# Sampling offsets of a deformable convolution: grid added by a matmul, copies merged, products and batch norm operations reordered

## The reference

```
out = relu(group_norm(conv1x1(x, w1)))                 # 64 channels
om  = conv3x3(out, w_off, pad=1) + b_off               # 27 channels
off_x, off_y, mask = om[:, :9], om[:, 9:18], sigmoid(om[:, 18:])
py = grid_y + off_y ; px = grid_x + off_x              # grid: pixel + tap offset
sampled = bilinear_sample(out, py, px) * mask          # 9 taps per pixel
out = relu(group_norm(einsum(sampled, w2)))
x = relu(group_norm(conv1x1(out, w3)) + x)
...
_bn(x, g, b, m, v):  inv = g * rsqrt(v + eps);  x * inv + (b - m * inv)
```

## Time and profile before

| what | value |
|---|---|
| median of 3 runs | 91.75 us (91.61 to 92.53) |
| the profiled execution | 92.51 us |
| its span in the trace | 90.7 us |
| mean granted TensorE clock | 0.987 |
| busy: PE / DVE / ACT / POOL | 75.6 / 65.4 / 50.7 / 5.0 us |
| busy: PE's weight loads | 51.2 us |

### The profile page before, as it was taken

How to read it: one execution, slowest core, us unless ns; L and a number is a source line. 1 busy time by engine, 2 the same in 40 slices (tenths; PEclk the granted TensorE clock), 3 DMA queues, 4 the chain that set the end, 5 groups by cost and what they waited for, 6 DMA issues and landing times.

```text
span 90.7 us, 2168 instructions
## 1 busy us (share of the span) xinstructions
PE 75.6 (83%) x885; PEld 51.2 (56%) x885; DVE 65.4 (72%) x178; ACT 50.7 (56%) x91; POOL 5.0 (6%) x10
## 2 busy tenths in 40 slices
PE   4999999996899898999999998979579877776400
PEld 1325665565699797799896975443224474552100
DVE  1125449999999699996699617988884884848950
ACT  4101374779957999994874014509380254735760
POOL 7500110000000000000001300000000000000000
PEclk9999999999999999999999999999999999999995
DMA  2999800000000000000000000000000000000076
GB/s 27 311 322 316 335 3 0 0 7 0 0 7 0 0 7 0 4 11 0 0 7 0 0 0 7 0 0 0 0 0 0 0 0 0 0 11 0 0 248 215
DMA packets 3274, 4.17 MB, mean 46 GB/s; under 512 B 256, under 2 KB 2688, under 8 KB 3264
## 3 DMA queue, kind: packets, MB, share of 16 engines
q1 hardware_dynamic: 2992, 3.76, 12.8%
q10 hardware_dynamic: 272, 0.26, 0.8%
HBM read 2.98 MB, written 1.05 MB: 44 GB/s over the span
## 4 chain that ended last, share of the span: by engine, by line
PE 52%; DVE 29%; ACT 11%; issue 4%; DVEq 0%; ACTq 0%
PE acc L482 15%; PE slot L469 9%; DVE g_rows L893 8%; PE slot L361 6%; PE acc L609 5%; PE acc L372 3%; ACT g_cols L794 3%; PE slot L397 3%; PE acc L588 3%; ACT g_cols L707 2%; DVE g_cols L1039 2%; PE slot L546 2%; ACT pad L760 2%; DVE g_cols L992 2%; DVE stats L956 2%
## 5 line engine op out<-in xcount | busy, mean ns | idle before, releaser
L893 DVE TENSOR_TENSOR g_rows<-hats 128x2304 f32<-128x2304 f32 (+1 forms) x12 | 20.6, 1753 | 0.1
L707 ACT ACTIVATE g_cols<-slot 128x768 f32<-128x768 f32 x24 | 17.8, 830 | 3.7 <-PE slot L469 3.7
L482 PE MATMUL acc<-g_cols,v_sb 128*64 128x128 f32 x288 | 17.9, 276 | 0.0
L361 PE MATMUL slot<-zeros 128*128 128x512 bf16 x58 | 16.1, 412 | 1.2 <-DVE zeros L813 1.2
L482 PEld LDWEIGHTS acc<-g_cols,v_sb 128*64 128x64 f32 x288 | 15.5, 137 | 1.1 <-issue 0.3
L469 PE MATMUL slot<-consts_sb,g_rows 64*128 64x64 f32 x288 | 11.8, 226 | 2.1 <-DVE g_rows L893 1.7
L469 PEld LDWEIGHTS slot<-consts_sb,g_rows 64*128 64x128 f32 x288 | 10.3, 140 | 3.9 <-DVE g_rows L893 2.6
L361 PEld LDWEIGHTS slot<-zeros 128*128 128x128 bf16 x58 | 5.8, 108 | 8.0 <-issue 2.9
L760 ACT ACTIVATE pad<-g_cols 64x256 bf16<-64x256 int8 x8 | 3.3, 418 | 5.5 <-DVE g_cols L1039 5.4
L824 DVE BATCH_NORM_STATS2 stats<-acc 128x6 f32<-128x256 f32 x4 | 1.7, 430 | 5.1 <-PE acc L372 2.7
L397 PE MATMUL slot<-feat,woff_sb 128*64 128x256 f32 x36 | 4.7, 385 | 0.0
(11 more groups left out here) (140 smaller groups left out, 115.7 us busy)
## 6 DMA issues: line engine op xcount, KB each, us to landing
out<-g_cols SPq DMA_DIRECT2D x4, 256.0 KB, 2.3
x_sb<-x SPq DMA_DIRECT2D x3, 256.0 KB, 4.2
wq_sb<-wq SPq DMA_DIRECT2D x1, 484.5 KB, 5.9
woff_sb<-woff SPq DMA_DIRECT2D x1, 288.0 KB, 5.1
w_sb<-w SPq DMA_DIRECT2D x1, 288.0 KB, 5.2
x_sb<-x ACTq DMA_DIRECT2D x1, 256.0 KB, 3.3
w_sb<-w SPq DMA_DIRECT2D x1, 256.0 KB, 6.1
consts_sb<-consts SPq DMA_DIRECT2D x1, 232.0 KB, 5.1
```

What stands on the lines that cost most here:

```text
L361: nc.tensor.matmul(bank, zeros[:, 0:P], zeros[:], start=True, stop=True)
L482: mm = nc.tensor.matmul(acc[b2][rows(h), at:at + P], v_sb[:, B2 * h + b2, q, k, :], g_cols[t][h][:, NQ * k + q, :], start=(k == 0 and q == ...
L707: nc.scalar.activation(dst.rearrange("p k (r n) -> p k r n", r=HALVES), src.rearrange("p r (k n) -> p k r n", k=per), ACT.Copy).then_inc(g ...
L893: tt(g_rows[i % 3][:, taps], hats[:, t, h, 1, taps].unsqueeze(3).to_broadcast(shape), hats[:, t, h, 0, taps].unsqueeze(2).to_broadcast(sha ...
```

## The change

- `grid_sb` gets 128 partitions. The grid's DMA fills the first 64, a DVE memset at the start zeroes the others (new semaphore `grid_zero`).
- In step s = 4 of `om_step` a tenth product `fold` x `grid_sb` is put beside the ninth tap, in partitions 64 to 127. It ends that accumulation.
- `add_grid` (DVE) and `copy_om_rest` (ACT) go. One ACT instruction, `copy_om`, copies all 128 partitions with the bias and gives `om_ready`; `om_rest_ready` goes.
- PE waits for the grid, its zeros and the constants ahead of the first offset step, not later.
- PE's order: `make_v(0)` and `make_v(1)` stand ahead of steps 2 to 4 of the second half instead of behind them. On ACT, `copy_om(1)` stands behind `copy_v(1)`.
- Four idle products between `turn(2)` and `turn(3)` (behind a wait for `v_ready` 8, which is met), and three between `sample(0, 0, 4)` and `turn(6)`.
- The six batch norm instructions move on DVE from behind `add_grid(0)` to behind `pair_scale(3, 0)`, ahead of the weights' quantisation.

```diff
@@ PE
-                                              stop=(k in (TAPS_A - 1, TAPS - 1)))
+                                              stop=(k == TAPS_A - 1))
+                    else:
+                        mm = nc.tensor.matmul(slot[0][CB * p:CB * p + CB, BANK * b2:BANK * b2 + N],
+                                              fold, grid_sb[:, N * b2:N * b2 + N], start=False, stop=True)
...
-                pe.wait_ge(om_rest_ready, b2 + 1)
...
             pe.wait_ge(woff_in, 16)
-            for b2 in range(B2):
-                pe.wait_ge(feat_ready, b2 + 1)
-                for s in range(TAPS_A):
-                    mm = om_step(b2, s)
-                    if b2 == 1 and s == 1:
-                        pe.wait_ge(consts_in, 16)
-                        om_turn(0)
-                mm.then_inc(om_done, 1)
+            pe.wait_ge(grid_in, 16)
+            pe.wait_ge(grid_zero, 1)
+            pe.wait_ge(consts_in, 16)
+            pe.wait_ge(feat_ready, 1)
+            for s in range(TAPS_A):
+                mm = om_step(0, s)
+            mm.then_inc(om_done, 1)
+            pe.wait_ge(feat_ready, 2)
+            om_step(1, 0)
+            om_step(1, 1)
+            om_turn(0)
...
-            for i in range(4):
-                make_v(i)
+            make_v(0)
+            make_v(1)
+            for s in range(2, TAPS_A):
+                mm = om_step(1, s)
+            mm.then_inc(om_done, 1)
+            make_v(2)
+            make_v(3)
             om_turn(1)
...
-            turns(0, 5)
+            turns(0, 2)
+            pe.wait_ge(v_ready, 2 * T)
+            idle(4, acc[1][:])
+            turns(3, 5)
             sample(0, 0, 4)
+            idle(3, acc[1][:])
             turns(6, 8)
@@ ACT
-            def copy_om_rest(b2):
+            def copy_om(b2):
                 a.wait_ge(om_done, b2 + 1)
-                nc.scalar.activation(om_sb[CB:P, N * b2:N * b2 + N], slot[0][CB:P, BANK * b2:BANK * b2 + N],
-                                     ACT.Copy).then_inc(om_rest_ready, 1)
+                nc.scalar.activation(om_sb[:, N * b2:N * b2 + N], slot[0][:, BANK * b2:BANK * b2 + N],
+                                     ACT.Identity, bias=vec[:, V_BOFF:V_BOFF + 1]).then_inc(om_ready, 1)
...
-            copy_om_rest(0)
+            copy_om(0)
             nc.scalar.preload_act_table(ACT.Sigmoid)
             make_mask(0)
-            copy_om_rest(1)
             for i in range(2 * T):
                 copy_v(i)
+                if i == 1:
+                    copy_om(1)
@@ DVE
+            nc.vector.memset(grid_sb[CB:P], 0.0).then_inc(grid_zero, 1)
...
-            dve.wait_ge(grid_in, 16)
             dve.wait_ge(consts_in, 16)
-            add_grid(0)
-
-            dve.wait_ge(bn_std_ready, 1)
-            (the six batch norm instructions, L901 to L907)
...
             make_hats(0)
-            add_grid(1)
             apply_mask(0)
...
             pair_scale(3, 0, V_GN2S, V_GN2B)
+            dve.wait_ge(bn_std_ready, 1)
+            (the same six)
+
             dve.wait_ge(wq_in, 16)
```

More of the change, by code:

```diff
@@ L140, in build @@
         woff_sb = sb("woff_sb", [P, TAPS, CB])
-        grid_sb = sb("grid_sb", [CB, PIX])
+        grid_sb = sb("grid_sb", [P, PIX])
         w2_sb = sb("w2_sb", [P, TAPS * CB])
@@ L223, in build @@
         pads_zero = sem("pads_zero")
+        grid_zero = sem("grid_zero")
         bn_var_ready = sem("bn_var_ready")
@@ L237, in build @@
         om_ready = sem("om_ready")
-        om_rest_ready = sem("om_rest_ready")
         omt_done = sem("omt_done")
@@ L326, in _ @@
             sp.dma_start(woff_sb[:], woff).then_inc(woff_in, 16)
-            sp.dma_start(grid_sb[:], grid).then_inc(grid_in, 16)
+            sp.dma_start(grid_sb[0:CB], grid).then_inc(grid_in, 16)
             sp.dma_start(consts_sb[:], consts).then_inc(consts_in, 16)
@@ L850, in _ @@
             pair_scale(2, 1, V_GN1S, V_GN1B)
[L852 to L857, removed]
             def differences(t):
@@ L942, in _ @@
             pair_scale(3, 0, V_GN2S, V_GN2B)
+            dve.wait_ge(bn_std_ready, 1)
+            settle(nc.vector.reciprocal(bn_std[:], bn_std[:]))
+            settle(tt(bn_inv[:], bn_std[:], vec[:, V_BNG:V_BNG + 4], ALU.mult))
+            settle(tt(bn_off[:], bn_inv[:], vec[:, V_BNM:V_BNM + 4], ALU.mult))
+            settle(tt(bn_off[:], vec[:, V_BNB:V_BNB + 4], bn_off[:], ALU.subtract))
+            settle(stt(bn_off[:, 0:1], bn_inv[:, 0:1], vec[:, V_PEGB:V_PEGB + 1], bn_off[:, 0:1], ALU.mult, ALU.add))
+            settle(ts(bn_minus[:], bn_off[:, 0:2], -1.0, None, ALU.mult))
             dve.wait_ge(wq_in, 16)
```

## The result

Slower. Four executions of the changed kernel had a median of 94.58 us, four of before 91.94: ratio 1.026, interval 1.021 to 1.032. The profiled execution took 94.54 us with a span of 92.7, against 92.51 and 90.7. A second set gave 94.62 us and 1.024 (1.019 to 1.029). Some executions of every kernel lose 1 to 2 us to a lower clock, and ratios leave out those more than 1.5% above the fastest of their kernel. The forecast was 93.3, range 92.0 to 94.2: right in direction and in most of its mechanisms, too low in size, and 94.58 lies outside the range.

The account below looks back on a forecast made before the run. It took ACT, without slack from 27.9 to 41.4 us, and two chains meeting at `turn(2)` as the bound. Terms -0.05 (V order), +0.85 (idle products), +0.72 (batch norm) gave +1.5 on 91.75: 93.3 us, range 92.0 to 94.2.

Parts of the forecast that it names:

- What bounds the kernel: At `turn(2)` DVE's products and ACT's V copies end within 0.02 us; a gain counts only if both get it.
- Copy with bias: Merged `om_sb` copy on ACT: 0.50 us, bounds 0.38 and 0.51; 0.47 by the skill's 93 ns per pointer operand.
- Grid product: PE, beside the ninth tap in the array's other 64 columns: costs nothing; alone, two passes of about 0.21 us per half.
- The three waits ahead of the first tap: PE's start: constants land at 9.3, first tap starts at 10.01; a margin of 0.7 us hides the waits, cost nothing.
- Two V products ahead: PE and ACT before `turn(2)`: same PE work in another order; `turn(2)` 0.05 us earlier, bounds 0.6 earlier to 0.3 later.
- the bound of 0.3: Late bound for `turn(2)`: 0.3 us later if the bias copy of half 1 holds V2's copy back on ACT.
- the sign of being right: Named beforehand as showing the forecast right: `turn(2)` starts within 0.15 us of 22.18.
- Idle products: PE between `turn(2)` and `turn(6)`: four cost ACT 0.15 to 0.2 us, three cost 0.76; +0.85 for both, bounds 0 and 1.7.
- Batch norm moved: DVE before the weights' quantisation: 1.13 us less 0.41 slack delays PE at `eight_means(0)` by 0.72 us, bounds 0.5 and 1.15.
- rival A: One cost is hidden, either the idle products or the batch norm: time 92.5 us, chance 0.23.
- Base: The loss is added to the 91.75 us median of three runs, 0.76 below the profiled execution of 92.5 us.
- Rival D: New wait at `eight_means` drops the clock to 1.2 GHz: 96 us, chance 0.04; alternatively idle products protect the turns' clock.

Follow-up runs that it names:

- experiment 6: Against before: merged copy and grid product only; no idle products, old V order, three waits ahead of the ninth tap, batch norm in DVE's idle wait before `pair_var(3, 0)`: 0.999.
- experiment 4: Changed kernel with the V products and second offset copy back in the old order: ratio to before 1.023, 94.40 us; the traced execution took 96.43 us.
- experiments 3: Changed kernel with the six batch norm instructions back at their early place on DVE: ratio to before 1.015.
- 11: Changed kernel without the three idle products ahead of `turn(6)`: one execution, 93.65 us, only its trace used; `turn(6)` 5.32 us behind `turn(2)`.
- number 8: Kernel of experiment 6 with `turn(6)` to `turn(8)` moved ahead of taps 3 and 4 of the first sample: ratio to before 1.009.
- number 13: Before with only two idle products added in PE's wait ahead of the last pair sums: ratio 1.000 to before.

## Why the prediction was wrong in size

- **What bounds the kernel.** Right: `turn(2)` waited for ACT's last V copy, and DVE's gain didn't count (experiment 6: 0.999). The changed trace names ACT for the same wait. `make_g(0)` came 0.5 us earlier, 0.6 was forecast.
- **Copy with bias.** 0.47 us measured, 0.50 taken. By the step for a pointer operand in the Trainium skill ("ScalarE: Activation LUTs", What ACT_TABLE_LOAD costs) it came to 0.47, and the trace agrees with that. Grid product: beside the ninth tap at no cost, as said.
- **The three waits ahead of the first tap, put at nothing.** The margin of 0.7 us was one trace's. The constants landed 5.1 to 6.0 us after their issue in the traces, and the first norm's end moved too. The waits cost nothing in the first trace of the changed kernel, 0.15 us in the second and 0.34 in that of experiment 4.
- **Two V products ahead, the first step that failed.** The sum had -0.05 us, on "PE's work is the same, in another order". The order has a price: `turn(2)` came at 22.39, 0.2 late. I read in the earlier trace rows how long a group took and not how long it took behind a group of its own kind. It lay inside the bound of 0.3, but for another reason than the one named, and past the 0.15 us named as the sign of being right.
- **Idle products, the second step that failed, in size.** Right in mechanism, +0.85 taken, +1.02 measured. The three cost 0.76 as forecast; the four cost 0.27, not 0.15 (`turn(3)` at 23.88, not 23.5). The forecast's own terms, 0.15 and 0.76, add up to 0.91, not 0.85.
- **Batch norm moved.** +0.72 taken, +0.77 measured, PE's wait 0.69 us where 0.6 to 0.8 was forecast. So rival A, one of the two costs hidden, is out: both were paid (experiments 3 and 11).
- **Sum.** 1.5 against 2.0 us: 0.24 from the V order (+0.19 for -0.05), 0.17 from the idle products, 0.05 from the batch norm.
- **Base, the step that put the number outside the range.** "I add to the median": the three runs' 91.75 lay 0.8 us below what later sets gave, and the profiled 92.51 was the typical execution. The measured 2.0 on 91.75 is 93.8, inside the range; the 0.8 us that the base lacked carries it out. The forecast 1.5 on the profiled execution gives 94.0; with 2.0 it is 94.5, as measured.
- **Rival D** didn't come about in the profiled execution of the changed kernel, and neither did the protection: without the seven idle products the clock in the turns stayed at 1.00. The rule on transposes in the Trainium skill ("TensorE: Matmul & The Clock Gate", PE-mode transpose) decided nothing here; turns and samples alternate, so no run tests it by itself. The place was right: the clock fell behind `eight_means` in number 8 and in the trace of number 4. The price, 96, was near too: that execution took 96.43 us, and two of the ten of the changed kernel, at mean clocks of 0.966 and 0.940, took 95.97 and 96.79. But number 8 has no wait at `eight_means`, and its clock fell all the same, so that the new wait is the cause isn't shown.

## What to carry to other kernels

Before you count on a wait that ends at one engine's event, look for every semaphore that the waiting instruction needs; where two end within 0.02 us of each other, the trace names only one. Instructions that are needed late go into an idle stretch of their engine that the trace shows (here 1.5 us on DVE ahead of `pair_var`), not merely later: the same six cost nothing there (experiment 6) and 0.77 us a little further on. And a few runs' median is not the profiled execution: find out which of the two is the odd one before you add to it.

## What was not expected of the hardware

- The start alone differs between executions of one kernel: the first convolution took 1.98 or 1.50 us, and the first tap was at 10.01 or 9.54, in two traces of before. Over the traces of all kernels here the first tap lies between 9.26 and 10.48 us. Not all of that is the clock: in the trace of number 13 PE waited 0.49 us for x to land. That the start makes up the whole spread of before's times (most between 91.7 and 92.8 us) isn't shown.
- A gain of about 0.9 us at `turn(6)` turned into a loss of 0.9%, because in all six executions the mean granted clock was lower; two more matmuls of zeros (under 0.5 us, in a wait) made it a gain of 1.1%. Why this arrangement of PE's work lets the clock fall every time stays open. Before does it seldom: 7 of the 80 executions in the later sets had a mean clock of 0.968 or less, and before with the same fill was unchanged (number 13), one of its 12 at 0.967.
- Here matmuls of one kind in a row were cheaper than the same ones in two groups: 3.36 against 3.56 us for the same work.
